# A second layer's cross-attention rebuilt to stay on chip, in a two-layer transformer block

## The reference

```python
def fq_sym(x):                       # 8 bits, one step for the whole tensor
    delta = jnp.maximum(jnp.max(jnp.abs(x)), 1e-08) / 127
    return jnp.clip(jnp.round(x / delta), -128, 127) * delta
def fq_zero(x):                      # for the softmax weights, in [0, 1]
    delta = jnp.maximum(jnp.max(x), 1e-08) / 255
    return jnp.clip(jnp.round(x / delta), 0, 255) * delta
def attention(x, ctx, Wq, Wk, Wv, Wo, bo, heads):
    q, k, v = fq_sym(x @ Wq), fq_sym(ctx @ Wk), fq_sym(ctx @ Wv)   # then split by heads
    w = fq_zero(softmax(q @ k.T * dh ** -0.5))
    return (w @ v) @ Wo + bo
```

## Time and profile before

| | us |
|---|---|
| median of 3 runs | 3719.68 (3715.29 to 3727.21) |
| the profiled execution's own time | 3716.17 |
| span of its trace | 3714.4 |
| PE busy | 2975.6 (80%), weight loads 1854.4 beside it |
| DVE busy | 2303.9 (62%) |
| ACT busy | 1916.2 (52%) |
| POOL busy | 724.2 (19%) |

### The profile page before, as it was taken

One profiled execution on the slowest core, in us unless ns is written; L12 is line 12 of the kernel. 1 busy time (PEld: TensorE's weight loads), 2 busy tenths in 40 slices (PEclk: granted clock), 3 DMA queues, 4 the chain that ended last, 5 costly groups with the idle time before them and its releaser, 6 DMA issues. The chain is left out here.

```text
span 3714.4 us, 51380 instructions
## 1 busy us (share of the span) xinstructions
PE 2975.6 (80%) x16324; PEld 1854.4 (50%) x16324; DVE 2303.9 (62%) x4118; ACT 1916.2 (52%) x3264; POOL 724.2 (19%) x1076
## 2 busy tenths in 40 slices
PE   5989999776969999979599996897750217699999
PEld 3744444464548888858111111223640104488888
DVE  4668888465533444346699996886653866344443
ACT  3438888532533323235599997996322325232322
POOL 1021111334440000000453511002330205300000
PEclk8979999887989999989555555666975559799999
DMA  6643333244730000015765436672324103201000
GB/s 182 208 143 105 104 108 105 63 117 127 184 88 18 9 17 8 0 57 153 175 156 115 114 63 88 79 98 48 89 75 152 28 11 73 45 17 32 16 23 15
DMA packets 477771, 307.04 MB, mean 83 GB/s; under 512 B 304150, under 2 KB 415982, under 8 KB 476942
## 3 DMA queue, kind: packets, MB, share of 16 engines
q1 hardware_dynamic: 471230, 288.64, 33.0%
q0 software_dynamic: 4240, 14.10, 1.3%
q10 hardware_dynamic: 2112, 1.97, 0.3%
HBM read 183.70 MB, written 118.78 MB: 81 GB/s over the span
## 5 line engine op out<-in xcount | busy, mean ns | idle before, releaser
L2053 DVE TENSOR_REDUCE neg_max<-nat 128x1 f32<-128x512 f32 x640 | 400.7, 682 | 65.0 <-PE nat L1919 64.9
L2248 PE MATMUL nat<-k_stack,q_stack 48*128 48x512 bf16 x640 | 380.7, 604 | 71.5 <-DMA k_stack<-k1w 30.8
L2282 DVE TENSOR_REDUCE m_all<-nat 128x1 f32<-128x512 f32 x640 | 423.3, 690 | 17.4 <-PE nat L2248 17.1
L2302 ACT ACTIVATE nat<-nat,m_all 128x512 f32<-128x512 f32 x640 | 427.7, 2129 | 2.3 <-DVE m_all L2282 2.3
L2302 ACT ACTIVATION_READ_ACCUMULATOR nat<-nat,m_all 128x1 f32 x640 | 403.7, 1674 | 0.0
L937 DVE SCALAR_TENSOR_TENSOR ff<-outp,bias,gel 128x512 f32<-128x512 f32 x160 | 120.1, 751 | 427.8 <-PE outp L407 427.8
L1992 ACT ACTIVATE probs<-sT 128x1024 f32<-128x1024 f32 x320 | 327.9, 1026 | 89.9 <-PE sT L1928 80.3
L2479 ACT ACTIVATE exps<-sT 128x1024 f32<-128x1024 f32 x320 | 296.3, 1083 | 15.6 <-PE sT L2419 13.7
L868 ACT ACTIVATE gel<-outp,bias 128x512 f32<-128x512 f32 x160 | 110.0, 687 | 360.6 <-PE outp L407 360.6
L749 POOL TENSOR_TENSOR rstd<-var_eps,neghalf 128x4 f32<-128x4 f32 x48 | 49.2, 1025 | 1147.6 <-DVE var_eps L919 1147.5
L872 ACT CAST ff_hi<-ff 128x512 fp32r<-128x512 f32 x160 | 99.2, 620 | 312.0 <-DVE ff L937 312.0
(11 more groups left out here) (444 smaller groups left out, 7000.5 us busy)
## 6 DMA issues: line engine op xcount, KB each, us to landing
v<-vpad SPq DMA_DIRECT2D x64, 320.0 KB, 2.8
q_stack<-q_part SPq DMA_DIRECT2D x90, 160.0 KB, 5.8
k_stack<-k1w SPq DMA_DIRECT2D x90, 160.0 KB, 10.6
q_stack<-q_hi SPq DMA_DIRECT2D x160, 64.0 KB, 2.5
k_stack<-k_hi SPq DMA_DIRECT2D x160, 64.0 KB, 2.2
v_stack<-v SPq DMA_DIRECT2D x40, 256.0 KB, 3.1
self_out<-o_nat SPq DMA_DIRECT2D x80, 128.0 KB, 2.0
attn_nat<-self_out SPq DMA_DIRECT2D x64, 160.0 KB, 2.9
```

The lines of the kernel that those rows point to most:

```text
L2053: dve.tensor_reduce(neg_max[:, n % 2, qt, 2 * pr + ab:2 * pr + ab + 1], nat[(16 * (n + 2) + t) % 3][:, :], AX.X, ALU.max, negate=True).the ...
L2248: pe.matmul(bank[i % NAT][:, :], q_stack[half, slot, g, pr, qt * P:(qt + 1) * P], k_stack[half, slot, g, pr, :], start=True, stop=True).th ...
L2282: dve.tensor_reduce(k.m_all[:, column(i // TILES, i % TILES)], bank[i % NAT][:, :], AX.X, ALU.max, negate=True).then_inc(s["e_max_ready"], 1)
L2302: act.activation(b[:, :], b[:, :], ACT.Exp, bias=k.m_all[:, col], accum_out=k.s_all[:, col]).then_inc(s["a_nat_free"], 1)
```

## The change

1. `context_phase` runs once, at the opening, for both layers. `first_loads` also loads and splits Wk2 and Wv2 of layer 1; seven more products give `k1` and `v1`, ACT copies them out, DVE takes their absolute maxima into `k.ctx_amax`, SP stores them as K21 by features (320 x 512) and V21 by tokens.
2. The phases for weights, context, steps, quantising, stats, weight step and attention of layer 1's cross-attention go, with `Stacks` and `Chain`. `exact_cross_attention` takes their place. It loads q by features and rounds it on chip into `q_int`; `k_int` holds 8 heads x 64 keys a tile block-diagonally, so one matmul with K = 128 gives eight heads' scores.
3. First half: per unit PE makes scores, DVE takes the grouped maxima, POOL splits these into hi and lo, PE makes the same scores again and adds the negated maxima by matmuls of an identity, ACT applies exp, POOL adds the two halves of each group, DVE sums; `nat`, `low`, `ex`, `halves`, `hi` and `lo` are double buffers. DVE places k (`place_k`, one piece for each of the three tiles) before units 0, 1 and 2. POOL's loader splits Wo2 and the first 256 rows of Wff2 in between (4 jobs of W = 160).
4. Second half: log-sums and maxima become three bf16 parts, PE turns them into `shift_rows` on chip (no DRAM trip), a 24-row matmul with `sel` adds them to the scores; exp, rounding, two column-tiled products (three units behind the scores), scaling, one store by features per tile.
5. `exact_self_attention` scales its output by features and stores four pieces of 16 rows a quad; no transposes.
6. `dense_phase` has `by_feature=True` for layer 1's "q" and "ff": three loads a sample, no `oT` transposes, ACT and DVE read the loaded tile in SBUF.
7. The rest of Wff2 (rows 256 to 1280, 6 jobs of W = 160) is split by POOL in the last "ff" phase, behind its bias additions and ahead of `rstd` of sample 0.

The core of the diff:

```diff
 def context_phase(...):
+                for m, M in enumerate(FEAT_TILES):
+                    sp.wait_ge(s["c_out1"], b["c_out1"] + m + 1)
+                    sp.dma_start(K21[m * P:m * P + M, :], k1[0:M, m, :]).then_inc(s["c_stored"], 16)
+                sp.wait_ge(s["c_out1"], b["c_out1"] + 3 + TT)
+                sp.dma_start(V21.rearrange("(t p) c -> p t c", p=P), v1[:, :, :]).then_inc(s["c_stored"], 16)
...
+                for m, M in enumerate(FEAT_TILES):
+                    if m:
+                        pe.wait_ge(s["c_out"], b["c_out"] + m)
+                    product(pe, k1_bank[m][0:M, :], wk1, slice(m * P, m * P + M), hi, lo,
+                            slice(0, TOK), False).then_inc(s["c_prod1"], 1)
...
 def dense_phase(...):
+                def load_attn_T(b, split_b=None):
+                    if split_b is not None:
+                        sp.wait_ge(s["oT_split"], at["oT_split"] + split_b * 3 + 3)
+                    src = rows(attn_in, b * D, D)
+                    sp.dma_start(attn[:, 0:2, :], src[0:2 * P].rearrange("(c p) t -> p c t", p=P)
+                                 ).then_inc(s["attn_in_loaded"], 16)
+                    for half in range(2):
+                        sp.dma_start(attn[64 * half:64 * half + 64, 2, :], src[2 * P:D]).then_inc(s["attn_in_loaded"], 16)
...
+                if main == "ff" and loader:
+                    for i in range(len(loader.jobs) + 1):
+                        loader.turn(pool, i)
+                    loader.passed()
...
+                        if loader and isinstance(b, int) and b == 0 and m == ws[1].full:
+                            pe.wait_ge(s["pool_split"], loader.split0 + len(loader.jobs))
...
+                        src = attn[:, m, :] if by_feature else bank_of(st, r)[:, :]
+                        act.copy(oT_hi[:, m, :], src).then_inc(s["oT_hi_done"], 1)
...
 def exact_self_attention(...):
-                            sp.dma_start(rows(out, (n - 2) * TOK, TOK).rearrange("(t p) c -> p t c", p=P),
-                                         o_nat[:, n % 2].rearrange("p t h c -> p t (h c)")
-                                         ).then_inc(s[f"a_o_stored{n % 2}"], 16)
+                            for h in range(4):
+                                sp.dma_start(rows(out, (n - 2) * 64 + h * DH, DH), o_sb[VCOL * h:VCOL * h + DH, n % 2, :]
+                                             ).then_inc(s[f"a_o_stored{n % 2}"], 16)
...
+                        dve.tensor_scalar(o_sb[:, n % 2, :], o_ps[n % 2][:, :], k.out_step, None, ALU.mult
+                                          ).then_inc(s["a_o_scaled"], 1)
...
+def exact_cross_attention(nc, s, k, q, kk, v, out, next_weights):
...
+                    def scores(bank, u, start):
+                        tile, half = tile_of(u), half_of(u)
+                        for i in range(2):
+                            qt = 2 * half + i if feats(tile) == P else 2 * i
+                            mm = pe.matmul(bank[:, i, :], q_int[:, tile, qt * P:(qt + 1) * P],
+                                           k_int[:, tile].rearrange("p h j -> p (h j)"), start=start, stop=True)
+                        return mm
+                    def natural(u):
+                        wait(pe, "y_max", u - 1)
+                        scores(nat[u % 2], u, True).then_inc(s["y_nat_full"], 1)
+                    def lowered(u):
+                        wait(pe, "y_exp", u - 1)
+                        for name, part in (("y_hi", hi), ("y_lo", lo)):
+                            wait(pe, name, u + 1)
+                            for i in range(2):
+                                pe.matmul(low[u % 2][:, i, :], identr[:, :],
+                                          part[:, u % 2, VH * i:VH * i + VH].unsqueeze(2).broadcast_to([P, VH, CTX_TOK]),
+                                          start=(part is hi), stop=False)
+                        scores(low[u % 2], u, False).then_inc(s["y_lowered"], 1)
+                    for u in range(-1, UNITS):
+                        if u + 1 < UNITS:
+                            natural(u + 1)
+                        if u >= 0:
+                            lowered(u)
...
+                    def place_k(m):
+                        for h in range(VH):
+                            ins = dve.tensor_scalar(dst[:, m, h], src, mask[:, h:h + 1], None, ALU.mult)
...
+                    for u in range(UNITS + 1):
+                        if u < UNITS:
+                            wait(pool, "y_max", u + 1)
+                            wait(pool, "y_lowered", u - 1)
+                            mine, r = columns(k.m_all, u), u % 2
+                            pool.tensor_copy(hi[:, r, :], mine).then_inc(s["y_hi"], 1)
+                            wait(pool, "y_hi", u + 1)
+                            pool.tensor_tensor(lo[:, r, :], mine, hi[:, r, :].bitcast(F32), ALU.subtract
+                                               ).then_inc(s["y_lo"], 1)
+                        if u >= 1:
+                            wait(pool, "y_exp", u)
+                            wait(pool, "y_summed", u - 2)
+                            e = ex[:, (u - 1) % 2, :].rearrange("p (x j) -> p x j", j=CTX_TOK)
+                            pool.tensor_tensor(halves[:, (u - 1) % 2, :].rearrange("p (x j) -> p x j", j=CTX_TOK // 2),
+                                               e[:, :, 0:CTX_TOK // 2], e[:, :, CTX_TOK // 2:CTX_TOK], ALU.add
+                                               ).then_inc(s["y_halved"], 1)
+                        loader.turn(pool, u)
...
+                        for i in range(2):
+                            j = 2 * half + i
+                            pe.matmul(sT[u % TURNS][:, i, :], k_int[:, tile, 2 * j:2 * j + 2, :].rearrange("p a j -> p (a j)"),
+                                      q_int[:, tile, :], start=True, stop=False)
+                            mm = pe.matmul(sT[u % TURNS][:, i, :], 
+                                           sel[row:row + ROWS, 2 * j:2 * j + 2, :].rearrange("p a j -> p (a j)"),
+                                           shift_rows[row:row + ROWS, batch, :], start=False, stop=True)
...
 def transformer(...):
-            steps_phase(nc, s, k)
-            quantise_phase(nc, s, k, [(q21, q21w, 0), (k21, k21w, 1), (v21, v21w, 2)])
-            stats_phase(nc, s, k, True, [q21w], [k21w], next_weights=[wo2, w2])
-            weight_step_phase(nc, s, k)
-            attention_phase(nc, s, k, 1, True, [q21w], [k21w], v21w, cross_out)
+            wo2 = Split(nc, s, own, "Wo2", w["Wo2"], over=wq)
+            w2 = [Split(nc, s, own, "Wff2", rows(w["Wff2"], 0, 2 * P), over=wo)]
+            exact_cross_attention(nc, s, k, q21, k21, v21, cross_out_T, [wo2, *w2])
+            w2.append(Split(nc, s, own, "Wff2", rows(w["Wff2"], 2 * P, FF - 2 * P)))
+            dense_phase(nc, s, k, 1, "ff", w["ln3_g"], w["ln3_b"], [w1, *w2], wo2, w["bo2"], cross_out_T,
+                        ff_bias=(w["bff1"], w["bff2"]), final=out.rearrange("b t c -> (b t) c"),
+                        next_weights=w2[1:], by_feature=True)
```

More of the change, by code:

```diff
@@ L458, in _ @@
             def _(pe):
-                pe.wait_ge(s["c_loaded"], b["c_loaded"] + (32 if ctx_nat is None else 0))
+                pe.wait_ge(s["c_loaded"], s.before("c_loaded"))
                 for c in range(2):
@@ L477, in _ @@
                     act.copy(hi[:, c, :], bank[c][:, :]).then_inc(s["c_hi"], 1)
-                if layer == 0:
-                    for m, M in enumerate(FEAT_TILES):
-                        act.wait_ge(s["c_prod"], b["c_prod"] + m + 1)
-                        act.copy(k_hi[0:M, m, :], bank[2 + m][0:M, :]).then_inc(s["c_khi"], 1)
+                for m, M in enumerate(FEAT_TILES):
+                    act.wait_ge(s["c_prod"], b["c_prod"] + m + 1)
+                    act.copy(k_hi[0:M, m, :], k_bank[m][0:M, :]).then_inc(s["c_khi"], 1)
+                for m, M in enumerate(FEAT_TILES):
+                    act.wait_ge(s["c_prod1"], b["c_prod1"] + m + 1)
+                    act.copy(k1[0:M, m, :], k1_bank[m][0:M, :]).then_inc(s["c_out1"], 1)
+                for t in range(TT):
+                    act.wait_ge(s["c_prod1"], b["c_prod1"] + 3 + t + 1)
+                    act.copy(v1[:, t, :], v1_bank[t][:, 0:D]).then_inc(s["c_out1"], 1)
             @block.vector
@@ L514, in context_phase @@
+                for t in range(TT):
+                    dve.wait_ge(s["c_out1"], b["c_out1"] + 3 + t + 1)
+                    dve.tensor_reduce(k.ctx_amax[:, 1, t:t + 1], v1[:, t, :], AX.X, ALU.max, apply_absolute_value=True)
+        for x, n in (("c_turned", 2), ("c_hi", 2), ("c_lo", 2), ("c_prod", 7), ("c_khi", 3), ("c_out", 7), ("c_vset", 2),
+                     ("c_prod1", 7), ("c_out1", 7), ("c_absmax", 1)):
             s.passed(x, n)
 def dense_phase(nc, s, k, layer, main, ln_g, ln_b, ws, wo=None, out_b=None, attn_in=None,
-                ff_bias=None, stores=None, final=None, next_weights=()):
```

(7 more changed lines are left out.)

1166 lines of the change are left out of this document (403 added, 763 removed).

## The result

The changed kernel takes 3595.19 us (median of four runs; one of them took 5308.7 and is left out of the comparisons, the other three lie at 3586.68, 3591.06 and 3599.32). The ratio to the kernel before is 0.9654, with a 95% interval of 0.9625 to 0.9683: some 125 us less. Forecast were 3518.5 and a range of 3460 to 3605; the time lies inside, near its upper end, and the gain is 62% of what was forecast. The profiled execution took 3591.06, its span is 3589.3, 125.1 less than before.

What follows compares the result with a forecast made beforehand. PE paces only the feed-forward, ACT the self-attention's second half; no engine is full in the replaced stage. Stage -218.5, elsewhere +4.6 -1.5 +4 +10.2, total -201.2 us: span 3513.2, median 5.3 above span, 3518.5; range 3460 to 3605.

Steps and rivals of the forecast that it cites:

- main case: Whole kernel: the forecast terms hold, giving 3518.5 us, own range 3495 to 3540; chance 0.60.
- Before the first unit, first half, loader: New cross-attention: 17.1 us before its first unit, 88 for 40 first-half units at 2.2, 13 for POOL's loader turns.
- The ring: Cross-attention's first half: POOL's hi/lo, PE's scores, ACT's exp and POOL's halves wait on each other, 2.17 us a unit.
- The rival of a slower first loop: Cross-attention's first half: loader and DVE/POOL contention stretch the period to 2.8, costing 24 us, total 3542; chance 0.12.
- Between the halves: Cross-attention, between its two halves: bf16 copies, transposes, block change and landing of v take 17 us (12 to 24).
- Second half: Cross-attention's second half: 40 units at 1.15 us with PE warm, 46 us (41 to 52).
- the clock rival: Both cross-attention halves: PE's clock falls, costing 49 and 39 us, total up to 3606; chance 0.14.
- The 10 for cold matmuls: Cross-attention stage: 5 us for cold matmuls after each pause, 5 for DVE and POOL in each other's way.
- Self-attention's end: Self-attention's second half: nothing from 40 quads; the last quad's turn and normalising fall away, -1.5 us.
- Dense q: Layer 1's dense q phase: dropped transposes gain nothing, oT_lo may slow beside POOL's additions, +4 us (-4 to +12).
- Feed-forward: Last feed-forward: transposes -9.6, POOL's six loader turns +19.6, earlier bias additions -2.2, contention +2.4; +10.2 us.
- Opening: Kernel's opening: splitting two more weights 2.4, four more stores on SP's queue 2.2; +4.6 us.

Runs made afterwards that it cites:

- e1b_sel128: Changed kernel with both second-half sel matmuls at 128 rows (zero-padded sel) in place of 24, `rest` placed in o_sb's memory; 3549.65 us.
- e2_osb4: Changed kernel with four o_sb output buffers in place of two in the self-attention's second half; 3557.26 us.
- e11_half: Changed kernel with the first of a unit's two second-half sel matmuls at 128 rows and the second at 24; 3555.60 us.
- e8_prebias: Changed kernel with POOL's output-bias additions moved ahead, into the second halves of the self-attention and cross-attention; 3565.28 us.
- e4_nobias: Changed kernel without POOL's eight output-bias additions in the two by-feature dense phases, so the output lacks these biases; 3556.69 us.
- e7_all: Changed kernel with 128-row sel, four o_sb buffers, new POOL orders in dense q and feed-forward, four opening stores on ACT's queue; 3500.54 us.
- e10_best2: e7_all with dense q's bias additions made by POOL at the end of the self-attention's first half; 3484.80 us.
- e9_best: e7_all with the bias additions placed as in e8_prebias instead of the new POOL orders, and the feed-forward's loader behind the first rstd; 3515.60 us.

## Why the prediction came out as it did

The direction and the range held; the predicted gain of 201 was 125. The main case, which had 0.60 and its own range of 3495 to 3540, did not: the time lies 55 above it. The range held because it reached up to the full loss of the clock, 3606, and the time came near that by two things: half of that rival at a higher price, and waits in the self-attention that no case held. That the number fell inside is so in part luck. By its own steps:

*Before the first unit, first half, loader: right.* From the stage's first load to the last exp of the first half 118.4 us were measured. The forecast's terms for the same stretch (17.1, 39 x 2.2, 13, and some 2 for the first unit's way to its exp) give 118. The distance is 2.30 in the steady state (2848.45 to 2859.95 is five units), against 2.2; the loader and the start cost 97.8 - 39 x 2.30 = 8.1 against 13. place_k took 2.30 and 3.31 for eight pieces, a little under the 3.5 taken. The ring was the bound, as said: DVE 83.9 and PE 84.9 of 104, none full. The rival of a slower first loop, 2.8 a unit, didn't come; the 2.81 that it quotes from the earlier trace rows is an operation of DVE's, not of POOL's.

*Between the halves: right.* 20.7 against 5.5 + 17.

*Second half: wrong, and the largest term.* The step that failed is "PE warm needs six matmuls, two of them side by side: 5 x 0.213 = 1.07, cold 2.13" with 1.15 taken. The clock was at its lower level, and each of the five steps cost 0.11 more than at that clock, since no weight load hid between matmuls of 24 and of 128 rows. 2.64 a unit: 57 us more than the 46. It was the clock rival, which had 0.14, in the second half alone, and dearer than its 39. (At the full clock the step would have been missed too: 1.29 a unit in e1b_sel128 without its pauses, not 1.07, as the loads around the products don't hide.) No case looked at the row counts. The rule of the Trainium skill that the rival names (TensorE: Matmul & The Clock Gate, section A second HAM failure mode: psum-queue depth-cycling) would have the first half swing between the levels. The traces don't agree: that half pauses in each unit and stands at 1.00 from 2835 to 2910, while the second is busy 100.6 of 103 and stands at 0.50. What the runs show is that with two 24-row matmuls in five steps the clock, once low, doesn't come back (80 us in e2_osb4), and with none or one it does (e1b_sel128, e11_half); the fall itself came in pauses (e2_osb4, e8_prebias). The trace of before held a sign that wasn't read so: the self-attention, whose score matmuls have 48 and 51 rows, is the stage with 0.50 and 0.65 at PE busy 89% and 87%, and the old attention phase with 128-row matmuls is the one at 0.94. For the self-attention this stays an inference; no run changed its rows. And one stage speaks against a rule by rows alone: layer 0's self-attention has score matmuls of 48 and 51 rows too, in fp32r, and from 400 to 550 of the changed kernel's trace PE is busy 146.2 of 150 us there at 1.00.

*Drain 5: 8.1 measured as tail.* The 10 for cold matmuls and for DVE and POOL in each other's way came from no row, and no run prices them by themselves.

*Self-attention's end: wrong.* "So does SP's work on four 16-row stores a quad in place of one: nothing from 40 quads" failed. Not the number of stores counted but what stands behind their buffer: DVE's wait for a store that lands 14 us late now stands ahead of the roundings. Six waits, 29.4 us of DVE; the exps 20.3 longer, 26.7 back by two more buffers. In the kernel before, the slowest store landed 14.3 us after its issue as well, and DVE waited 1.4 for stores in all; why it was so little there no run asks. Work taken off the path was costed, a wait added to an engine's queue was not.

*Dense q: direction right, size off.* 8.4 for 4, inside -4 to +12. The reason is POOL's additions beside DVE's passes with two SBUF inputs: three oT_lo of sample 0 take 9.73, three of sample 1 8.57, and e4_nobias takes 12.0 away with the additions. By the rule of the Trainium skill (GPSIMD Engine Reference, section 8, Key points) the forecast had some +8, by longer oT_lo in all samples. The kind and the size agree, the place doesn't: behind the two first samples, once the additions are over, an oT_lo takes 0.69.

*Feed-forward: right.* 8.8 for 10.2, the loader 18.4 for 19.6 (six turns of 3.2 are 19.2), with DVE waiting 22.2 for rstd. PE's busy time behind it is 7.0 less for 9.5: 72 transposes fewer in that stretch, not 96, as those of the first samples lie ahead of it.

*Opening: right in kind.* 2.6 by the splits (v stores start at 37.61, not 35.05) and 3.3 by four stores behind them, 5.8 for 4.6. On ACT's queue it was 48.8 in e7_all and 51.6 in e10_best2, so not clearly less.

## What to carry to other kernels

Price a matmul by the shape of its weights as well as its columns: where the shape changes from one matmul to the next, the weight load showed in the distance here (0.11), and with two 24-row bf16 matmuls in five steps the loop stayed at the low clock; padding with zeros to 128 rows gave 44 us for 3 KB of memory a partition. Look at the clock of such a loop before believing the price. When stores replace an on-chip step, ask who waits for their buffer and what stands behind that wait, above all where big loads share the queue. Big additions on POOL belong beside DVE passes that read PSUM, or into a stage where DVE isn't the pace.

## What the runs showed of the hardware

- With PE busy 80 of 80 us the granted clock stood at 0.50 (e2_osb4, two 24-row matmuls in five steps), with 16 to 17.5 of 20 at 1.00 (e1b_sel128, none). A full engine isn't enough for the full clock.
- The fall to 0.50 came in a pause of PE: 0.99 us in e2_osb4, 2.69 in e8_prebias. Pauses of 1.23 in e1b_sel128 left the clock at 1.00; in e9_best, with waits of up to 4.72, it fell twice and came back both times (no 24-row matmuls there).
- A weight load isn't hidden between matmuls of 24 and of 128 rows, nor between weights of 32 and of 128 columns: 0.11 at the low clock (0.535 for 0.43), 0.10 to 0.11 at the full one (0.31 to 0.33 for 0.215). Between equal shapes it is (1.03 for two at the low clock).
- POOL's 128x1280 additions stretch DVE's passes from SBUF to two to five times: oT_lo 0.69 to 3.36 at most, z 0.60 to 1.13 on average, roundings 0.69 to 3.37 at most. A pass from PSUM beside them stays at 0.74, and the maxima from PSUM keep their pace (none of the 640 over 0.693 in e10_best2).
- A store queued behind large loads landed 14.4 us after its issue, where 1.7 is the median (the changed kernel's self-attention).
